# Inverse row sums turned together with the row maxima, from batch two on

## The chip, the cores and the metric

One core of a Trainium2 chip runs the kernel. The metric is the device time of one execution in microseconds (us). The core has five engines that work in their own order and wait for each other by semaphores: TensorE (PE in the rows, its weight loads PEld), VectorE (DVE), ScalarE (ACT), GpSimd (POOL) and SyncE (SP), which issues the transfers.

## The reference

Four batches of 512 tokens with 512 channels go through one layer: causal cross attention to a 128-wide context (16 heads in 4 groups, 32 wide), and then a mixture of eight units with a shared branch. The attention is what the change touches:

```python
scores = jnp.einsum('bgnqd,bgkd->bgnqk', qg, k) * scale
scores = jnp.where(causal, scores, -1e30)
attn = jax.nn.softmax(scores, axis=-1)
out = jnp.einsum('bgnqk,bgkd->bgnqd', attn, v)
out = out.reshape(B, N_HEADS, T, hd).transpose(0, 2, 1, 3).reshape(B, T, C)
return out @ w_out.T
```

## The kernel before, in words

The attention is cut into 32 spans `u`: batch `b` (4), half of the queries `h` (2), key group `kv` (4). A span has 4 heads (`G`) of 256 queries (`Q`), which is 2 tiles of 128 queries per head. Spans 0 to 7 are the first batch, 8 to 31 the other three.

Each engine runs one hand-written loop over the same 288 slots `s`, from -40 to 247. In every slot it issues its share of that slot's work in a fixed order. `span_slot(u)` is the slot at which span u starts. From batch two on a span takes 4 slots when h is 0 and 8 or 9 when h is 1. Nearly all slots from 32 on also hold one "filler": one 128 x 512 product of the mixture, of the output projection or of the down projection, in two parts of six or more fp32r matmuls, and two PSUM banks (`u_bank`) take turns at them.

Softmax is done in two passes. In the first pass (`pass_a`, line 1510) queries are the rows: in the slots of the span before u, DVE takes each row's maximum (`row_max`, 1227) and ACT the exponentials' row sums (`row_sum`, 980). In the second pass (`pass_b`, 1534) keys are the rows, and the negated maxima must stand along the queries as two more rows of `q_st`. So

- DVE splits the maxima into a high and a low fp32r part (`maxima_split`, 1236 and 1238, into `mhl`) at slot `span_slot(u) - 1`;
- PE turns them (`maxima_turn`, 1490) at slot `span_slot(u)`, behind the first part of the filler and the slot's `pass_a` products, and ahead of the filler's second part;
- ACT copies them to `m_t` (`maxima_out`, 972), and SP carries them to `q_st` (`rows`), which the second pass reads from slot `span_slot(u) + 3`.

The inverse row sums scale the value products, whose rows are 32 channels of each of 4 heads. So

- DVE takes the reciprocal (`inverse`, 1244) near the end of slot `span_slot(u)`;
- POOL spreads each head's value over 32 columns (`spread_inverse`, 872, into `rrep`) one slot later;
- PE turns both 128 x 128 tiles (`inverse_turn`, 1499) first thing in slot `span_slot(u) + 5`, and ACT copies them to `r_t` (`inverse_out`, 987), for DVE's `attended` (1253).

Small products share a ring of three PSUM banks (`short_products`): one may start when the bank's reader three products ago is done.

In a slot DVE's order is: the first row maximum, the low part of a turned tile (1205), the evacuation of the filler of slot s - 1 (`gate` with 1366 and 1387 for a unit, `residual` ending in 1266, or `finish`, 1398), the other row maxima, and then all else. The gate waits for ACT's tanh of the same filler (1048). ACT's tanh of the filler of slot s - 1 stands early in its slot s, behind all of its slot s - 1, which ends with `weights_high` (945).

Of the kernel before, what the change touches and what calls it, by code (L numbers as in the profile page):

```python
# [70 lines left out]
def attention_and_mixture_kernel(nc, x, ctx_in, q_norm_w, k_norm_w, w_out, w_router, w_units, w_down,  # L71
# [38 lines left out]
    U0 = 3  # L110
    POOL_LOW = (3,)

    f32 = lambda ap: ap.bitcast(F32)
# [6 lines left out]
    with common:  # L120
# [42 lines left out]
        wt = sb("wt", [P, NT, NK])  # L163
        st2, mv2, ln2 = sb("st2", [P, NT, 6]), sb("mv2", [P, NT, 2]), sb("ln2", [P, 4, NT])
        mixs, amp = sb("mixs", [NE, NK]), sb("amp", [NE, NK, 2])
# [25 lines left out]
        def sem(name):  # L191
# [31 lines left out]
        s_pa, s_max, s_sum, s_mhi, s_mlo, s_mt, s_mout = (sem(n) for n in (  # L223
            "pass_a", "row_max", "row_sum", "max_high", "max_low", "max_turned", "max_out"))
        s_rinv, s_rrep, s_rt1, s_rout = (sem(n) for n in (
            "row_inverse", "inverse_spread", "inverse_turned", "inverse_out"))
# [73 lines left out]

        def of_span(s, name):
# [265 lines left out]
        def short_products(s):  # L567

            found = []
            if (u := of_span(s, "inverse_turn")) is not None:  # L570
# [72 lines left out]
        def sync_engine(e):  # L643
# [48 lines left out]
            def rows(u):  # L692
                e.wait_ge(s_mout, u - KV + 1)
                if u >= QR:
                    e.wait_ge(*queries_read(u - QR))
                for k in range(2):
                    e.dma_start(f32(q_st[MAXROW + k:MAXROW + k + 1, u % QR, :, :]),
                                f32(m_t[k * G:(k + 1) * G, :])).then_inc(s_m[u % 2], 16)

# [61 lines left out]
        def pool_engine(e):  # L761
            e.memset(half_neg[:], -0.5).then_inc(s_small, 1)
            e.memset(ident[:], 0.0)
# [4 lines left out]
            e.affine_select(out=ident[:], in_=ident[:], compare_op=ALU.not_equal, fill=1.0, base=0,  # L768
                            pattern=[[-1, P]], channel_multiplier=1)
# [98 lines left out]
            def spread_inverse(u):  # L868
                e.wait_ge(s_rinv, u + 1)
                if u >= 1:  # L870
                    e.wait_ge(s_rt1, u)
                e.tensor_copy(heads(rrep[:]), rinv[:, u % 2].unsqueeze(3).broadcast_to([P, TH, G, D])
                              ).then_inc(s_rrep, 1)

            def mask_probabilities(u, k):

# [32 lines left out]
            for s in slots:  # L909
                if (step := second_pass_step(s - SELECT)) is not None:  # L910
                    mask_probabilities(*step)
                if (hb := of_half(s, "query_scale")) is not None:
                    query_scale(hb)
                if (u := of_span(s, "spread")) is not None:
                    spread_inverse(u)
# [26 lines left out]
        def scalar_engine(e):  # L942
# [25 lines left out]
            def maxima_out(u):  # L968
                e.wait_ge(s_mt, u - KV + 1)
                if u > KV:  # L970
                    e.wait_ge(*max_rows(u - 1))
                e.activation(m_t[:], short("maxima", u - KV)[0:2 * G, 0:Q], ACT.Copy).then_inc(s_mout, 1)

# [94 lines left out]
            for s in slots:  # L1068
# [4 lines left out]
                for n in tiles_in(s, "turn"):  # L1073
                    high(n)
                if (u := of_span(s, "inverse_turn")) is not None:
                    inverse_out(u)
# [33 lines left out]
        def vector_engine(e):  # L1110
# [119 lines left out]
            def maxima_split(u):  # L1230
                r = u % 2
                hi, lo = mhl[:, r, :, 0:G], mhl[:, r, :, G:2 * G]
                e.wait_ge(s_max, (u + 1) * G * TH)
# [22 lines left out]
            def residual(f):  # L1256
# [6 lines left out]
                e.wait_ge(s_x1, n + 1)  # L1263
                e.bn_stats(st2[:, n, :], xs).then_inc(s_bn2, 1)
                e.wait_ge(s_bn2, n + 1)
                e.bn_aggr(mv2[:, n, :], st2[:, n, :]).then_inc(s_agg2, 1)

# [139 lines left out]
            for s in slots:  # L1407
# [39 lines left out]
                for g in moments_in(s):  # L1447
                    moments(g)
                if (u := of_span(s, "inverse")) is not None:
                    inverse(u)  # L1450
# [9 lines left out]
        def tensor_engine(e):  # L1460
# [3 lines left out]
            def turn_in(n):  # L1464
# [4 lines left out]
                for t in range(TH):  # L1469
                    last = e.transpose(bank[:, t * P:(t + 1) * P], r1_b[:, n % 2, t, :], ident[:])  # L1470
                last.then_inc(s_turn, 1)

            def turn_stacked(n):
# [3 lines left out]
                for i, done in enumerate((s_turn_a, s_turn)):  # L1477
                    e.wait_ge(*stack_free(n, i))
                    for j in range(2):
                        for t in range(TH):  # L1480
                            copies = r3[:, n % 2, t * G + 2 * i + j].rearrange("p c d -> p (c d)")
                            last = e.transpose(stack_banks(n)[i][0:MAXROW, j * Q + t * P:j * Q + (t + 1) * P], copies, ident[:])
                    last.then_inc(done, 1)

            def maxima_turn(u):
                e.wait_ge(s_mlo, u - KV + 1)
                e.wait_ge(*short_free("maxima", u - KV))
                bank = short("maxima", u - KV)
                for t in range(TH):
                    last = e.transpose(bank[0:2 * G, t * P:(t + 1) * P], f32(mhl[:, u % 2, t, :]), ident[:])  # L1490
                last.then_inc(s_mt, 1)

            def inverse_turn(u):

                e.wait_ge(s_rrep, u + 1)
                e.wait_ge(*short_free("inverse", u))
                bank = short("inverse", u)
                for t in range(TH):
                    last = e.transpose(bank[:, t * P:(t + 1) * P], rrep[:, t, :], ident[:])
                last.then_inc(s_rt1, 1)  # L1500
# [12 lines left out]
            def turn_probabilities(u, k):  # L1513
# [4 lines left out]
                for j in range(G):  # L1518
                    for t in range(k, TH):
                        at = j * w + t * P - seen(u, k)  # L1520
                        last = e.transpose(pair[:, at:at + P], masked_scores(u, j * TH + t)[:, k * P:(k + 1) * P], ident[:])
                last.then_inc(s_pb, 1)
# [30 lines left out]
            def turn_x(n):  # L1553
# [3 lines left out]
                for k in range(KC):  # L1557
                    last = e.transpose(bank[:, k * P:(k + 1) * P], xn[:, k * P:(k + 1) * P], ident[:])  # L1558
                last.then_inc(s_xt, 1)
# [13 lines left out]
            def turn_choice(p):  # L1573
# [3 lines left out]
                for t in range(2):  # L1577
                    last = e.transpose(bank[:, t * P:(t + 1) * P], cf[:, t, 0:NE], ident[:])
                last.then_inc(s_cft, 1)
# [10 lines left out]
            def turn_down(g):  # L1590
# [6 lines left out]
                for h in range(2):  # L1597
                    e.wait_ge(*short_free("down", 2 * g + h))
                    bank = short("down", 2 * g + h)
                    for k in range(ND // 2):  # L1600
                        last = e.transpose(bank[:, k * P:(k + 1) * P], blocks[h * (ND // 2) + k], ident[:])  # L1601
                    last.then_inc(s_dt, 1)
# [70 lines left out]
            for s in slots:  # L1673
                if (u := of_span(s, "inverse_turn")) is not None:
                    inverse_turn(u)
# [101 lines left out]
```

## Time and profile before

| | |
|---|---|
| median of 3 runs | 809.68 us (809.2 to 809.68) |
| the profiled execution's own time | 809.42 us |
| its span, first to last instruction | 807.7 us |
| PE busy | 763.8 us, 95% |
| PE weight loads | 608.0 us, 75% |
| DVE busy | 646.1 us, 80% |
| ACT busy | 578.0 us, 72% |
| POOL busy | 532.5 us, 66% |
| mean granted TensorE clock | 0.987 of 2.4 GHz |

Busy time is that of an engine with an instruction at work; for PE the ends of matmuls are modelled and overlap the next one's start, so the time from start to start says what one costs.

### The profile page before, as it was taken

To read this page: it belongs to the slowest core of one execution; us is meant where nothing else is said; L and a number is where in the kernel's file an instruction comes from. 1 tells how busy PE (TensorE), PEld (TensorE's weight loads), DVE (VectorE), ACT (ScalarE), POOL (GpSimd) and SP (SyncE) were. 2 spreads that over 40 slices of the span, in tenths; PEclk is the share of its full clock that TensorE was granted. 3 is DMA by queue.
4 is the path that set the end of the run, shared out by engine and by line. 5 is a ranking of instruction groups with operands and counts; after the bars stand their busy time and mean duration, and the time that the engine had idled before them with its cause. 6 is when DMAs were issued, how large, how long until landed. Compare 5 with 4: busy or idle time off the path is not lost. (4 is left out here: it accounts for less than half of the span.)

```text
span 807.7 us, 15292 instructions
## 1 busy us (share of the span) xinstructions
PE 763.8 (95%) x4180; PEld 608.0 (75%) x4180; DVE 646.1 (80%) x1635; ACT 578.0 (72%) x1413; POOL 532.5 (66%) x685
## 2 busy tenths in 40 slices
PE   2768799999999999999999999999999999999998
PEld 2545577777777878777778778777778887788886
DVE  7767787889788877889788787888788887688774
ACT  3878796788777867788778767787777775655552
POOL 4586489784697769775687849777465615662572
PEclk9979999999999999999999999999999999999999
DMA  8323144554545446545455445554545335454650
GB/s 291 122 68 97 41 134 161 179 166 138 192 156 172 153 141 220 194 154 178 146 175 179 141 157 181 170 164 135 197 150 173 136 125 185 157 188 133 207 201 35
DMA packets 57052, 127.03 MB, mean 157 GB/s; under 512 B 10920, under 2 KB 28040, under 8 KB 56968
## 3 DMA queue, kind: packets, MB, share of 16 engines
q1 hardware_dynamic: 56968, 126.04, 47.3%
q8 instruction: 36, 0.59, 0.3%
q14 instruction: 48, 0.39, 0.2%
HBM read 107.55 MB, written 4.46 MB: 139 GB/s over the span
## 5 line engine op out<-in xcount | busy, mean ns | idle before, releaser
L1634 PE MATMUL u<-w_h,t_h 128*128 128x512 f32 x640 | 258.4, 404 | 1.1 <-issue 0.8
L1634 PE MATMUL u<-w_l,t_h 128*128 128x512 f32 x640 | 251.2, 393 | 0.0
L1634 PE MATMUL u<-w_h,t_l 128*128 128x512 f32 x640 | 251.0, 392 | 0.0
L1284 DVE TENSOR_TENSOR w_l<-w_raw,w_h 128x512 fp32r<-128x512 f32 x288 | 240.4, 861 | 0.3 <-ACT w_h L945 0.3
L945 ACT ACTIVATE w_h<-w_raw 128x512 fp32r<-128x512 f32 x384 | 219.0, 621 | 7.9 <-DMA w_raw<-in_w_units 7.0
L899 POOL TENSOR_TENSOR w_l<-w_raw,w_h 128x512 fp32r<-128x512 f32 x96 | 139.1, 1449 | 101.8 <-ACT w_h L945 101.8
L980 ACT ACTIVATE scores<-scores,mx 128x384 f32<-128x384 f32 (+1 forms) x224 | 128.8, 575 | 70.4 <-DVE mx L1227 69.2
L907 POOL TENSOR_TENSOR macc<-macc,gb 128x256 f32<-128x256 f32 x112 | 106.1, 951 | 58.9 <-DVE gb L1387 58.4
L1634 PEld LDWEIGHTS u<-w_h,t_l 128*128 128x128 f32 x640 | 120.6, 188 | 26.9
L1227 DVE CUSTOM_DVE_ANT_0 scores<-s,mask_qk 128x384 f32<-128x384 f32 (+1 forms) x224 | 112.4, 503 | 35.5 <-PE s L1510 34.9
L1634 PEld LDWEIGHTS u<-w_h,t_h 128*128 128x128 f32 x640 | 121.0, 189 | 25.8 <-issue 3.0
L1634 PEld LDWEIGHTS u<-w_l,t_h 128*128 128x128 f32 x640 | 121.3, 190 | 20.1
L1510 PE MATMUL s<-k_st,q_st 96*128 96x384 f32 (+1 forms) x248 | 88.1, 366 | 8.2 <-DVE mx L1227 3.9
L998 ACT ACTIVATE pr<-pair 128x1024 f32<-128x1024 f32 x88 | 77.7, 883 | 21.1 <-PE pair L1534 20.6
L1366 DVE SCALAR_TENSOR_TENSOR th<-th,u 128x256 f32<-128x256 f32 x160 | 66.5, 416 | 31.9 <-ACT th L1048 30.0
L1048 ACT ACTIVATE th<-u 128x256 f32<-128x256 f32 x160 | 60.2, 376 | 36.2 <-PE u L1634 35.6
L882 POOL TENSOR_SCALAR_AFFINE_SELECT pr<-pr 128x512 f32<-128x512 f32 x56 | 47.2, 843 | 36.8 <-ACT pr L998 36.8
L1387 DVE SCALAR_TENSOR_TENSOR gb<-th,wt,u 128x256 f32<-128x256 f32 x112 | 53.9, 481 | 16.0
L1510 PEld LDWEIGHTS s<-k_st,q_st 96*128 96x128 f32 x248 | 48.2, 199 | 22.9 <-issue 14.8
L1534 PE MATMUL pair<-q_st,k_st 98*128 98x512 f32 x148 | 51.0, 410 | 2.0 <-ACT pr L998 2.0
L1549 PE MATMUL o_bank<-pr,ct 128*32 128x256 f32 (+1 forms) x768 | 42.6, 363 | 0.0
L980 ACT ACTIVATION_READ_ACCUMULATOR scores<-scores,mx 128x1 f32 x224 | 42.5, 190 | 0.0
(152 smaller groups left out, 1175.0 us busy)
## 6 DMA issues: line engine op xcount, KB each, us to landing
w_raw<-in_w_units SPq DMA_DIRECT2D x160, 512.0 KB, 4.2
w_raw<-in_w_out_t SPq DMA_DIRECT2D x16, 512.0 KB, 5.1
w_raw<-in_shared_w_down SPq DMA_DIRECT2D x16, 512.0 KB, 4.6
q_st<-turned_h SPq DMA_DIRECT2D x224, 32.0 KB, 2.8
out<-x SPq DMA_DIRECT2D x16, 256.0 KB, 2.2
q_st<-turned_l SPq DMA_DIRECT2D x112, 32.0 KB, 2.7
x<-in_x SPq DMA_DIRECT2D x3, 1024.0 KB, 9.2
k_st<-turned_h SPq DMA_DIRECT2D x48, 32.0 KB, 2.8
```

Source lines behind the costliest of these rows:

```text
L899: e.tensor_tensor(w_l[:, i % WR, k, :], w_raw[:, i % WR, k, :], f32(w_h[:, i % WR, k, :]), ALU.subtract).then_inc(s_wlp, 1)
L907: e.tensor_tensor(total, total, gb[:, adds_before(w, g) % 2, :], ALU.add).then_inc(s_acc, 1)
L945: e.activation(w_h[:, i % WR, k, :], w_raw[:, i % WR, k, :], ACT.Copy).then_inc(s_wh, 1)
L980: e.activation(s, s, ACT.Exp, bias=mx[:, u % 2, t, j:j + 1], scale=-1.0, accum_out=sums[:, u % 2, t, j:j + 1]).then_inc(s_sum, 1)
L998: e.activation(pr[:, n % PR, 0:width], pair[:, 0:width], ACT.Exp, scale=-1.0).then_inc(s_ex, 1)
L1048: e.activation(th[:, n % 2, :], u_bank[filler_no[f] % 2][:, 0:I], ACT.Tanh, scale=0.5).then_inc(s_tanh, 1)
L1227: e.tensor_tensor_reduce(masked_scores(u, m), scores_bank(i)[:, 0:width], mask_qk[:, T - width:T], 1.0, 3e38, ALU.add, ALU.min, mx[:, u % ...
L1284: e.tensor_tensor(w_l[:, i % WR, k, :], w_raw[:, i % WR, k, :], f32(w_h[:, i % WR, k, :]), ALU.subtract).then_inc(s_wl, 1)
L1366: e.scalar_tensor_tensor(th[:, n % 2, :], th[:, n % 2, :], 1.0, up, ALU.add, ALU.mult).then_inc(s_ga, 1)
L1387: e.scalar_tensor_tensor(to, th[:, n % 2, :], scale, gate_v, ALU.mult, ALU.mult).then_inc(s_gb, 1)
L1510: e.matmul(scores_bank(i)[:, 0:w], q_st[0:MAXROW, u % QR, j, t * P:(t + 1) * P], k_st[0:MAXROW, (b * KV + kv) % KR, 0:w], start=True, stop ...
L1634: last = e.matmul(u_bank[n % 2][:], t[:, k, cols], ww[:, i % WR, k, :], start=(k == 0 and m == 0), stop=(k == KC - 1 and m == 2))
```

## The change

Spans 0 to 7 keep the spread and the turn of full tiles. For spans 8 to 31:

- `mhl` is 16 wide: high and low part of the inverses (`hi`, `lo`, 4 columns each) stand ahead of those of the maxima. DVE does the reciprocal and then two more operations (`inverse_split`), now right behind the evacuation of the filler in slot `span_slot(u)`, ahead of the slot's other row maxima.
- `maxima_turn` waits for that split too and turns all 16 columns. For all spans from 4 on it is now an ordinary fp32r matmul with the unit matrix in place of a transposition. `maxima_out` copies 16 rows.
- `inverse_turn` is one fp32r matmul of a constant 0/1 matrix (`chooser`, 8 x 128) with the first 8 rows of `m_t`, at slot `span_slot(u) + 3` in place of + 5.
- POOL makes `chooser` once, in slot 53, and copies no more inverses. `st2` shrinks to two entries, with a wait.

```diff
+INVERSE_ROWS, CHOOSER_SLOT = 3, 53
+    SPREAD = H * KV
-        mhl, m_t = sb("mhl", [P, 2, TH, 2 * G], F32R), sb("m_t", [2 * G, Q], F32R)
-        rrep, r_t = sb("rrep", [P, TH, P]), sb("r_t", [P, 2, Q])
+        mhl, m_t = sb("mhl", [P, 2, TH, 4 * G], F32R), sb("m_t", [4 * G, Q], F32R)
+        chooser, r_t = sb("chooser", [P, TH, P], F32R), sb("r_t", [P, 2, Q])
-        ident = sb("ident", [P, P])
+        ident_r = sb("ident", [P, P], F32R)
+        ident = f32(ident_r[:])
...
+        def inverse_rows_in(s):
+            for u in range(SPREAD, NU):
+                if s == span_slot(u):
+                    return u
+            return None
+        def inverse_turn_in(s):
             for u in range(NU):
-                if s == span_slot(u) + core(u, name):
+                if s == span_slot(u) + (core(u, "inverse_turn") if u < SPREAD else INVERSE_ROWS):
                     return u
...
+            def make_chooser():
+                e.wait_ge(s_rt1, SPREAD)
+                rows = chooser[0:2 * G, 0, :]
+                e.memset(f32(rows), 0.0).then_inc(s_chooser, 1)
...
+                e.affine_select(out=by_head(rows), in_=by_head(f32(rows)), compare_op=ALU.not_equal, fill=1.0, base=0,
+                                pattern=[[-1, G], [0, D]], channel_multiplier=1).then_inc(s_chooser, 1)
...
             def maxima_out(u):
+                if u > SPREAD:
+                    e.wait_ge(s_rt1, u)
+                made = 2 * G if u < SPREAD else 4 * G
+                e.activation(m_t[0:made, :], short("maxima", u - KV)[0:made, 0:Q], ACT.Copy).then_inc(s_mout, 1)
...
             def inverse(u):
                 e.wait_ge(s_sum, (u + 1) * G * TH)
                 if u >= 2:
-                    e.wait_ge(s_rrep, u - 1)
+                    e.wait_ge(*((s_rrep, u - 1) if u - 2 < SPREAD else (s_isplit, 2 * (u - 1 - SPREAD))))
                 e.reciprocal(rinv[:, u % 2], sums[:, u % 2]).then_inc(s_rinv, 1)
+            def inverse_split(u):
+                r = u % 2
+                hi, lo = mhl[:, r, :, 0:G], mhl[:, r, :, G:2 * G]
+                e.wait_ge(s_rinv, u + 1)
+                if u >= KV + 2:
+                    e.wait_ge(s_mt, u - KV - 1)
+                e.tensor_copy(hi, rinv[:, r]).then_inc(s_isplit, 1)
+                e.wait_ge(s_isplit, 2 * (u - SPREAD) + 1)
+                e.tensor_tensor(lo, rinv[:, r], f32(hi), ALU.subtract).then_inc(s_isplit, 1)
...
                     evict[fillers[s - 1][0]](fillers[s - 1])
                 if s == START[0]:
                     mixture_table()
+                if (u := inverse_rows_in(s)) is not None:
+                    inverse(u)
+                    inverse_split(u)
                 for u, m in first_pass_tiles(s)[1:]:
                     row_max(u, m)
...
             def maxima_turn(u):
                 e.wait_ge(s_mlo, u - KV + 1)
+                if u >= SPREAD:
+                    e.wait_ge(s_isplit, 2 * (u - SPREAD) + 2)
+                first = 2 * G if u < SPREAD else 0
                 e.wait_ge(*short_free("maxima", u - KV))
                 bank = short("maxima", u - KV)
                 for t in range(TH):
-                    last = e.transpose(bank[0:2 * G, t * P:(t + 1) * P], f32(mhl[:, u % 2, t, :]), ident[:])
+                    last = e.matmul(bank[0:4 * G - first, t * P:(t + 1) * P], mhl[:, u % 2, t, first:4 * G], ident_r[:],
+                                    start=True, stop=True)
                 last.then_inc(s_mt, 1)
             def inverse_turn(u):
+                if u >= SPREAD:
+                    e.wait_ge(s_chooser, 3)
+                    e.wait_ge(s_mout, u - KV + 1)
+                    e.wait_ge(*short_free("inverse", u))
+                    e.matmul(short("inverse", u)[:, 0:Q], chooser[0:2 * G, 0, :], m_t[0:2 * G, :],
+                             start=True, stop=True).then_inc(s_rt1, 1)
+                    return
```

## Rows read from the trace of the kernel before

**Rows 1.** Stretch of batches two to four: busy us (x instructions) by engine, clock, DMA.

```profile
134.00:690.00 556.00, 551.79 (x3072) 442.63 (x3073) 462.55 (x1174) 421.32 (x1037) 385.85 (x480) 1.00 0.50 165
```

**Rows 2.** PE's longest wait in that stretch: us in total, times, longest.

```profile
PE s L1601 <- DVE mx L1227: 1.5, 3, 0.6
```

**Rows 3.** Timeline, spans 8, 16, 17, 18, 31: start us, duration us; filler's evacuation, maxima's turn.

```profile
136.32 0.38 PE L1490 MATMUL s<-ident,mhl 128*8 128x128 f32 x2
136.86 0.48 DVE L1387 SCALAR_TENSOR_TENSOR gb<-th,wt,u 128x256 f32<-128x256 f32 x1
...
323.25 0.48 DVE L1387 SCALAR_TENSOR_TENSOR gb<-th,wt,u 128x256 f32<-128x256 f32 x1
325.05 0.38 PE L1490 MATMUL s<-ident,mhl 128*8 128x128 f32 x2
...
338.14 0.38 PE L1490 MATMUL s<-ident,mhl 128*8 128x128 f32 x2
338.97 0.48 DVE L1387 SCALAR_TENSOR_TENSOR gb<-th,wt,u 128x256 f32<-128x256 f32 x1
...
352.10 0.38 PE L1490 MATMUL s<-ident,mhl 128*8 128x128 f32 x2
353.22 0.48 DVE L1387 SCALAR_TENSOR_TENSOR gb<-th,wt,u 128x256 f32<-128x256 f32 x1
...
676.83 0.48 DVE L1387 SCALAR_TENSOR_TENSOR gb<-th,wt,u 128x256 f32<-128x256 f32 x1
677.01 0.38 PE L1490 MATMUL s<-ident,mhl 128*8 128x128 f32 x2
```

**Rows 4.** Timeline of ACT ahead of span 18's turn.

```profile
350.87 1.15 ACT L945 ACTIVATE w_h<-w_raw 128x512 fp32r<-128x512 f32 x2
...
352.18 0.39 ACT L1048 ACTIVATE th<-u 128x256 f32<-128x256 f32 x1
```

**Rows 5.** Timeline of DVE: the two splitting operations of span 18's maxima.

```profile
350.17 0.17 DVE L1236 TENSOR_SCALAR mhl<-mx 128x8 fp32r<-128x8 f32 x1
350.38 0.17 DVE L1238 SCALAR_TENSOR_TENSOR mhl<-mx,mhl 128x8 fp32r<-128x8 f32 x1
```

**Rows 6.** Groups by line, shapes apart: busy us, mean ns of one, idle before and releaser.

```profile
L1238 DVE SCALAR_TENSOR_TENSOR mhl<-mx,mhl 128x8 fp32r<-128x8 f32 x28 | 11.2, 400 | 1.0
...
L1236 DVE TENSOR_SCALAR mhl<-mx 128x8 fp32r<-128x8 f32 x28 | 9.4, 337 | 0.5
...
L1244 DVE RECIPROCAL rinv<-sums 128x8 f32<-128x8 f32 x32 | 6.2, 195 | 1.4 <-ACT early L980 1.3
```

**Rows 7.** The same view of POOL.

```profile
L872 POOL COPY rrep<-rinv 128x256 f32<-128x256 f32 x32 | 17.3, 539 | 15.4 <-DVE rinv L1244 15.0
```

**Rows 8.** The same view of PE: the 128-column fp32 value products.

```profile
L1549 PE MATMUL o_bank<-pr,ct 128*32 128x128 f32 x256 | 13.6, 286 | 0.0
```

**Rows 9.** Timeline of PE: two products of a filler; two transpositions, then products.

```profile
405.83 0.39 PE L1634 MATMUL u<-w_l,t_h 128*128 128x512 f32 x1
406.06 0.39 PE L1634 MATMUL u<-w_h,t_l 128*128 128x512 f32 x1
...
406.74 0.38 PE L1470 MATMUL s<-ident,r_b 128*128 128x128 f32 x2
406.88 0.48 PE L1634 MATMUL u<-w_h,t_h 128*128 128x512 f32 x1
407.20 0.40 PE L1634 MATMUL u<-w_l,t_h 128*128 128x512 f32 x1
```

**Rows 10.** Timeline of PE: a 256-column fp32r product and the next.

```profile
334.16 0.28 PE L1510 MATMUL s<-k_st,q_st 96*128 96x256 f32 x1
334.28 0.39 PE L1534 MATMUL pair<-q_st,k_st 98*128 98x512 f32 x1
```

**Rows 11.** Two stretches of the first batch, columns as in the first group.

```profile
71.00:77.60 6.60, 5.32 (x32) 3.39 (x34) 5.42 (x16) 5.63 (x13) 3.65 (x9) 1.00 0.49 177
77.60:81.10 3.50, 3.50 (x34) 1.92 (x27) 2.20 (x6) 2.71 (x8) 3.00 (x8) 0.51 0.22 57
```

More of the change, by code:

```diff
@@ L140, in attention_and_mixture_kernel @@
         mx, sums, rinv = (sb(n, [P, 2, TH, G]) for n in ("mx", "sums", "rinv"))
-        mhl, m_t = sb("mhl", [P, 2, TH, 2 * G], F32R), sb("m_t", [2 * G, Q], F32R)
-        rrep, r_t = sb("rrep", [P, TH, P]), sb("r_t", [P, 2, Q])
+        mhl, m_t = sb("mhl", [P, 2, TH, 4 * G], F32R), sb("m_t", [4 * G, Q], F32R)
+        with ExitStack() as before:
+            rrep = before.enter_context(nc.sbuf_tensor("rrep", [P, TH, P], F32))
+        chooser, r_t = sb("chooser", [P, TH, P], F32R), sb("r_t", [P, 2, Q])
         o_h = sb("o_h", [P, KV, T], F32R)
         mask_qk = sb("mask_qk", [P, T])
-        ident = sb("ident", [P, P])
+        ident_r = sb("ident", [P, P], F32R)
+        ident = f32(ident_r[:])
         w_h, wd_h = sb("w_h", [P, WR, KC, 2 * I], F32R), sb("wd_h", [P, KD, C], F32R)
@@ L299, in maxima_in, with of_spread_span @@
             return u if u is not None and (u < H * KV) == first else None
-        def of_span(s, name):
+        def of_spread_span(s, name):
+            for u in range(SPREAD):
+                if s == span_slot(u) + core(u, name):
+                    return u
[3 more added lines that the diff above has]
+                if s == span_slot(u):
+                    return u
+            return None
+        def inverse_turn_in(s):
             for u in range(NU):
-                if s == span_slot(u) + core(u, name):
+                if s == span_slot(u) + (core(u, "inverse_turn") if u < SPREAD else INVERSE_ROWS):
                     return u
@@ L569, in short_products @@
             found = []
-            if (u := of_span(s, "inverse_turn")) is not None:
+            if (u := inverse_turn_in(s)) is not None:
                 found.append(("inverse", u))
@@ L695, in rows @@
                     e.wait_ge(*queries_read(u - QR))
+                first = 0 if u < SPREAD else 2 * G
                 for k in range(2):
                     e.dma_start(f32(q_st[MAXROW + k:MAXROW + k + 1, u % QR, :, :]),
-                                f32(m_t[k * G:(k + 1) * G, :])).then_inc(s_m[u % 2], 16)
+                                f32(m_t[first + k * G:first + (k + 1) * G, :])).then_inc(s_m[u % 2], 16)
             def store(g):
@@ L873, in spread_inverse @@
                               ).then_inc(s_rrep, 1)
+            def make_chooser():
+                e.wait_ge(s_rt1, SPREAD)
+                rows = chooser[0:2 * G, 0, :]
+                e.memset(f32(rows), 0.0).then_inc(s_chooser, 1)
+                by_head = lambda ap: ap.rearrange("p (j d) -> p j d", d=D)
+                e.wait_ge(s_chooser, 1)
+                e.affine_select(out=by_head(rows), in_=by_head(f32(rows)), compare_op=ALU.not_equal, fill=1.0, base=0,
+                                pattern=[[-1, G], [0, D]], channel_multiplier=1).then_inc(s_chooser, 1)
+                e.wait_ge(s_chooser, 2)
+                e.affine_select(out=by_head(rows), in_=by_head(f32(rows)), compare_op=ALU.not_equal, fill=1.0, base=-G,
+                                pattern=[[-1, G], [0, D]], channel_multiplier=1).then_inc(s_chooser, 1)
             def mask_probabilities(u, k):
@@ L913, in pool_engine @@
                     query_scale(hb)
-                if (u := of_span(s, "spread")) is not None:
+                if s == CHOOSER_SLOT:
+                    make_chooser()
+                if (u := of_spread_span(s, "spread")) is not None:
                     spread_inverse(u)
@@ L1074, in scalar_engine @@
                     high(n)
-                if (u := of_span(s, "inverse_turn")) is not None:
+                if (u := inverse_turn_in(s)) is not None:
                     inverse_out(u)
@@ L1231, in maxima_split @@
                 r = u % 2
-                hi, lo = mhl[:, r, :, 0:G], mhl[:, r, :, G:2 * G]
+                hi, lo = mhl[:, r, :, 2 * G:3 * G], mhl[:, r, :, 3 * G:4 * G]
                 e.wait_ge(s_max, (u + 1) * G * TH)
@@ L1448, in vector_engine @@
                     moments(g)
-                if (u := of_span(s, "inverse")) is not None:
+                if (u := of_spread_span(s, "inverse")) is not None:
                     inverse(u)
@@ L1469, in turn_in @@
                 for t in range(TH):
-                    last = e.transpose(bank[:, t * P:(t + 1) * P], r1_b[:, n % 2, t, :], ident[:])
+                    last = e.transpose(bank[:, t * P:(t + 1) * P], r1_b[:, n % 2, t, :], ident)
                 last.then_inc(s_turn, 1)
@@ L1481, in turn_stacked @@
                             copies = r3[:, n % 2, t * G + 2 * i + j].rearrange("p c d -> p (c d)")
-                            last = e.transpose(stack_banks(n)[i][0:MAXROW, j * Q + t * P:j * Q + (t + 1) * P], copies, ident[:])
+                            last = e.transpose(stack_banks(n)[i][0:MAXROW, j * Q + t * P:j * Q + (t + 1) * P], copies, ident)
                     last.then_inc(done, 1)
@@ L1498, in inverse_turn @@
                 for t in range(TH):
-                    last = e.transpose(bank[:, t * P:(t + 1) * P], rrep[:, t, :], ident[:])
+                    last = e.transpose(bank[:, t * P:(t + 1) * P], rrep[:, t, :], ident)
                 last.then_inc(s_rt1, 1)
@@ L1520, in turn_probabilities @@
                         at = j * w + t * P - seen(u, k)
-                        last = e.transpose(pair[:, at:at + P], masked_scores(u, j * TH + t)[:, k * P:(k + 1) * P], ident[:])
+                        last = e.transpose(pair[:, at:at + P], masked_scores(u, j * TH + t)[:, k * P:(k + 1) * P], ident)
                 last.then_inc(s_pb, 1)
@@ L1557, in turn_x @@
                 for k in range(KC):
-                    last = e.transpose(bank[:, k * P:(k + 1) * P], xn[:, k * P:(k + 1) * P], ident[:])
+                    last = e.transpose(bank[:, k * P:(k + 1) * P], xn[:, k * P:(k + 1) * P], ident)
                 last.then_inc(s_xt, 1)
@@ L1577, in turn_choice @@
                 for t in range(2):
-                    last = e.transpose(bank[:, t * P:(t + 1) * P], cf[:, t, 0:NE], ident[:])
+                    last = e.transpose(bank[:, t * P:(t + 1) * P], cf[:, t, 0:NE], ident)
                 last.then_inc(s_cft, 1)
@@ L1600, in turn_down @@
                     for k in range(ND // 2):
-                        last = e.transpose(bank[:, k * P:(k + 1) * P], blocks[h * (ND // 2) + k], ident[:])
+                        last = e.transpose(bank[:, k * P:(k + 1) * P], blocks[h * (ND // 2) + k], ident)
                     last.then_inc(s_dt, 1)
@@ L1673, in tensor_engine @@
             for s in slots:
-                if (u := of_span(s, "inverse_turn")) is not None:
+                if (u := inverse_turn_in(s)) is not None:
                     inverse_turn(u)
```

14 lines of the change are left out of this document (8 added, 6 removed).

## The prediction

> **What bounds the kernel now.** I read the table of stretches first, for the stretch in which spans 8 to 31 run. PE is at work for 551.8 of 556 us at full clock, while DVE has 462.6, ACT 421.3 and POOL 385.9 [rows 1]. The waits of PE come next: its longest in this stretch are three for a row maximum, 1.5 us together, 0.6 the longest [rows 2]. So PE sets the pace from 134 to 690 us. What another engine saves there is worth nothing, what PE saves is worth its start-to-start time, and whatever makes PE wait is added nearly whole, because PE has no idle time in which to take it back.
>
> The view that decides is the timeline around PE's turn of the maxima, since that is where the change adds a wait. The kernel before turns them as soon as PE comes to them; their split was made a slot earlier. What is new must wait for DVE to reach a later place in its queue: the evacuation of the filler of slot s - 1.
>
> **The new wait.** In slot `span_slot(u)` DVE now does, in this order: evacuate the last filler, reciprocal, copy, subtract. PE's turn in the same slot needs the last of them. Behind the turn in PE's queue stand the second-pass product of the slot and the second part of the filler, and everything after; none can pass.
>
> How late is DVE? At span 18 PE starts the turn at 352.10, and DVE's gate of the last filler runs from 353.22 to 353.70, 1.60 us behind PE's start [rows 3]. The reason is ACT: it makes two high parts of weights from 350.87 to 352.02, and its tanh of that filler starts only at 352.18, after PE had come to the turn [rows 4]. In the kernel before this lateness costs nothing, because only the next use of the filler's bank depends on it.
>
> From the gate's end the chain is: reciprocal 0.20 us [rows 6], then copy and subtract. Neither is in the trace on the inverses, but the maxima's split is the same pair of shapes: 0.17 each when undisturbed [rows 5], 0.34 and 0.40 in the mean [rows 6]. Between the two lie 0.04 us (350.17 + 0.17 to 350.38) [rows 5]; I take this for each of three hand-overs, the last to PE. That gives 0.20 + 0.34 + 0.12 = 0.66 at least and 0.20 + 0.74 + 0.12 = 1.06 with mean durations. I take 0.85.
>
> So PE's wait at a span is the evacuation's end + 0.85 - the turn's start, or nothing where that is negative [rows 3]:
> - span 8: 136.86 + 0.48 + 0.85 - 136.32 = 1.87
> - span 16: 323.25 + 0.48 + 0.85 - 325.05 < 0, nothing
> - span 17: 338.97 + 0.48 + 0.85 - 338.14 = 2.16
> - span 18: 353.22 + 0.48 + 0.85 - 352.10 = 2.45
> - span 31: 676.83 + 0.48 + 0.85 - 677.01 = 1.15
>
> The other 19 spans, read the same way, follow this pattern: spans 8 to 11, 17 to 19 and 25 to 27 wait 1.5 to 2.7, spans 12, 20 and 28 wait 0.8, spans 29 to 31 about 1.2, and the other eight 0.13 or nothing. The sums over the 24 pairs of such rows, from the first at 136.32 to the last at 677.01, are 8.8 us in batch two, 7.3 in three and 11.3 in four: 27.4. With a chain of 0.66 it is 24, with 1.06 about 32.
>
> Does a wait at one span make the next shorter, because ACT and DVE catch up? Partly. Span 16 has DVE in time and span 17, four slots later, has it late again by the full amount [rows 3]: the lateness is rebuilt within a span by the order in the slots, and is not a backlog carried from before. I take a tenth off, an estimate, for what ACT and DVE make up: 24.6 us.
>
> **PE's own work.** The time from start to start is the price. Two transpositions of 128 x 128 and one 512-column product take 407.20 - 406.74 = 0.46 us, and the product by itself takes 406.06 - 405.83 = 0.23: 0.115 for a transposition [rows 9].
> - Removed: 24 spans x 2 transpositions of `rrep` x 0.115 = 5.5 us.
> - Added: 24 products with the 0/1 matrix, 256 fp32r columns, 334.28 - 334.16 = 0.12 each [rows 10]: 2.9 us.
> - Changed: 28 x 2 = 56 turns of `mhl`, transpositions at 0.115, become fp32r products of 128 columns. No row shows such a product. Below it is bounded by half of the 256-column row, 0.06 [rows 10]; above by the fp32 value products of the same 128 columns, four of which run side by side in 13.6 / 64 = 0.21 us [rows 8]. Operands and width are those of the transpositions, so I keep their 0.115, and the term is nothing. The ends are 56 x (0.06 - 0.115) = -3.1 and 56 x (0.21 - 0.115) = +5.3 us.
>
> Together PE's work is 2.6 us less, between -5.7 and +2.7.
>
> The Trainium skill ("FP8 and Floating Point Precision", section "TensorE Precision Notes") says that a true fp32 product takes four passes through the array and that reduced precision reads 4 bytes and truncates. By one pass the new turns would cost the lower bound above, and the sum would be 3.1 us lower; no row here shows a narrow fp32r product, so the sum does not go by it.
>
> **What costs nothing.** POOL loses 24 copies of 0.54 us [rows 7] and gains three small operations in slot 53; it has 170 us idle in the stretch [rows 1], and before it no one waited for its copy at PE. DVE gains 48 operations of 0.17 to 0.40 us, up to 18 us in all, in its 93 idle us [rows 1]; uncovered, they are already in the wait's chain. They stand ahead of the slot's other row maxima, whose bank PE needs three small products later, and PE itself is later by then. ACT copies 16 rows in place of 8 with the same 256 columns. Nothing waits anew on SP: its two transfers of maxima rows wait for `maxima_out` as before, and the second pass that reads them stands three slots further on, over 10 us, so that neither they nor the weight loads behind them in SP's queue come late. The move of `inverse_turn` from slot + 5 to + 3 shifts the ring of banks by one place in two slots of each span; PE's three waits there of at most 0.6 [rows 2] say what such a collision costs, so I put at most 24 x 0.1 = 2.4 us in the range and nothing in the sum.
>
> **The sum.** 24.6 - 2.6 = +22.0 us on the profiled execution's 809.4 (its span of 807.7 and 1.7 around it) is 831.4; the median of the runs is 0.3 higher than that execution, so 831.7, say 832.
>
> **Rivals.**
> - *The clock falls too*, chance 0.2. In the first batch the granted clock went from 2.4 to 1.2 GHz for 3.5 us after 6.6 us in which PE worked 5.32, that is with 1.3 us idle [rows 11]. The new waits put up to 2.7 us of idle time into such a stretch, so some could bring a fall. Each costs half of 3.5 us, 1.7 us; with a fall at 6 of the 10 spans with waits over 1.5 us it is +10: 842. Against it, PE works at full density between the waits, which it did not in the first batch. The Trainium skill ("TensorE: Matmul & The Clock Gate", section "HAM oscillation — how this bites in real kernels") tells of kernels that lose the fast clock at each pause between dense groups; the trace has such falls only in the first batch.
> - *The lateness is a backlog*, chance 0.15: each wait lets ACT and DVE catch up and the next spans find them nearer. If half of the 27.4 us goes so, the time is 809.7 + 13.7 - 2.6 = 821. Span 17 speaks against it.
> - *Faster*, chance 0.04: the first waits, some 2 us, clear the lateness for good, and PE's work saves its lower bound 5.7; 809.7 + 2 - 5.7 = 806. It decides from the point at which all waits together are under the saving, 2.6 us in the middle case. At span 18 alone the wait is 2.45, so this needs ACT's tanh to move by over a microsecond at nearly all ten places.
> - *Waits and saving cancel*, chance 0.03: 809 to 811.
>
> **How the numbers follow.** The forecast has the remaining 0.58. Its own range takes the wait's ends (24 and 32, less a tenth: 21.6 to 28.8), PE's ends (-5.7 to +2.7) and the ring's 2.4: 809.7 + 15.9 = 825.6 to 809.7 + 33.9 = 843.6. The range for 8 in 10 reaches down to most of the backlog case and takes in the clock case's middle: 819 to 846. A difference of 0.2%, 1.6 us, is about what a measurement of this kernel can tell from none. Faster by more has 0.04, within it 0.03, slower 0.93.
>
> **What would show it.** In the changed kernel PE's waits should have a new first line: the turn of `mhl` waits for DVE's split of the inverses, about 18 times and 25 us in all, the longest near 2.5 us, at spans 9, 10, 17, 18, 25 and 26, and nearly none at 13, 15, 16, 21, 23 and 24. The stretch of batches two to four should be some 22 us longer with PE's idle time up by as much. Start-to-start times of the new 128-column turns would show 0.06, 0.115 or 0.21. Granted clock under 1.00 in that stretch would be the first rival; waits that shrink after the first span of a batch, the second. The prediction is wrong if DVE reaches the split less than a microsecond behind PE at most spans.

## The result and the profile after

The changed kernel takes 840.94 us (median of 6 runs, 839.29 to 844.64) against 809.68 (6 runs, 807.14 to 810.28): ratio 1.0403, 95% interval 1.0387 to 1.0418. The profiled execution took 840.38 us, its span is 838.7, 31.0 more than before. The forecast was 832, range 819 to 846, slower with 0.93. So the time lies in the range, 9 us above the forecast.

The stretch table of the changed kernel has the same columns as [rows 1]. It goes on to 720 us, where the changed kernel has done the work that the kernel before had done at 690:

```profile
134.00:720.00 586.00, 560.59 (x3049) 440.90 (x3048) 476.42 (x1219) 422.22 (x1036) 366.20 (x458) 1.00 0.48 156
```

PE was idle for 4 us of its stretch in [rows 1]; here it is idle for 25. The waits of PE over the whole span (us in total, times, longest) name the place:

```profile
PE s L1549 <- issue: 25.1, 16, 2.5
...
PE s L1577 <- DVE mx L1268: 3.2, 5, 1.3
```

L1549 is the turn of `mhl`. The view puts the wait down to "issue", that is to nothing that it could name. One version of the kernel (e4, below, which differs in the rows of another product) has the same waits, and for two of them its view names the releaser; L1296 is the subtraction in `inverse_split`:

```profile
PE s L1550 <- DVE mhl L1296: 5.0, 2, 2.5
```

The timelines of PE and DVE at span 18 of the changed kernel say the same. They answer to the fourth pair of rows in [rows 3] and to [rows 5]:

```profile
363.18 0.28 PE L1577 MATMUL s<-k_st,q_st 96*128 96x256 f32 x1
365.82 0.37 PE L1549 MATMUL s<-ident,mhl 128*16 128x128 f32 x2 [2.36 <-issue]
365.99 0.73 PE L1601 MATMUL pair<-q_st,k_st 98*128 98x512 f32 x1
```

```profile
363.53 0.42 DVE L1246 TENSOR_TENSOR turned_l<-s,turned_h 128x256 fp32r<-128x256 f32 x1 [1.46 <-ACT turned_h L998]
363.87 0.41 DVE L1419 SCALAR_TENSOR_TENSOR th<-th,u 128x256 f32<-128x256 f32 x1
364.43 0.48 DVE L1440 SCALAR_TENSOR_TENSOR gb<-th,wt,u 128x256 f32<-128x256 f32 x1
364.83 0.20 DVE L1285 RECIPROCAL rinv<-sums 128x8 f32<-128x8 f32 x1
365.06 0.24 DVE L1293 CAST mhl<-rinv 128x8 fp32r<-128x8 f32 x1
365.33 0.39 DVE L1295 TENSOR_TENSOR mhl<-rinv,mhl 128x8 fp32r<-128x8 f32 x1
```

DVE's gate ends at 364.91 and its subtraction at 365.72. The turn starts at 365.82, which is 0.91 us behind the gate's end, where 0.85 was assumed. Before the turn PE stands idle from the end of the score product to that moment.

A wait's idle time is a little less than what it costs, since a matmul's modelled end lies behind the moment at which the next could have started. The cost is the time from the start of the product ahead of the turn to the start of the turn: 365.82 - 363.18 = 2.64 here. Added over spans 8 to 31 it is 32.6 us in the changed kernel and 5.6 in the kernel before, 27.1 more.

The product with the 0/1 matrix at span 19, with its neighbours and two of the weight loads (PEld):

```profile
397.79 0.39 PE L1722 MATMUL u<-w_h,d_l 128*128 128x512 f32 x1
398.11 0.18 PEld L1559 LDWEIGHTS s<-m_t,chooser 8*128 8x128 f32 x1 [0.36 <-issue]
398.11 0.38 PE L1559 MATMUL s<-m_t,chooser 8*128 8x256 f32 x1
398.42 0.19 PEld L1577 LDWEIGHTS s<-k_st,q_st 96*128 96x128 f32 x1
398.42 0.44 PE L1577 MATMUL s<-k_st,q_st 96*128 96x384 f32 x1
398.70 0.40 PE L1722 MATMUL u<-wd_h,d_h 128*128 128x512 f32 x1
```

It starts 0.32 us behind the product before it, which alone takes 0.23, and the next starts 0.31 behind it, where 0.12 was forecast [rows 10]. Its weights and those of the next are loaded only as each product starts. Adding up start-to-start differences between the two kernels around the 24 old and the 24 new places of the inverse turn gives +5.7 us, where the forecast had 2.9 - 5.5 = -2.6. How far behind each place one counts matters a little: up to the second product behind it, the sum is +5.4, of which the 24 new products are 11.6 and the removed transpositions -6.2.

The two products of each new turn start 0.06 us apart, the lower bound of the forecast. But the products behind them come later by most of what this saves: from the start of a turn to the second product behind it the two kernels differ by 0.01 us in the mean. That is 0.3 us in all, and 1.0 us in a version without the wait (e12, below).

From 134 us to the last products the granted clock fell once, to 1.2 GHz, right at a wait. Stretch, busy us by engine, clock, DMA share, GB/s:

```profile
365.60:369.00 3.40, 3.18 (x9) 2.62 (x10) 2.20 (x5) 2.49 (x6) 3.26 (x6) 0.50 0.95 305
```

An estimate: 3.4 us at half the clock cost half of them, 1.7. Over the whole of a run, the mean granted clock was 0.988 in the fastest of the six (839.29 us) and 0.978 in the slowest (844.64 us).

### The profile page after: what moved, and what is told of

Read it like the earlier page. It is cut to its first block, busy times and chain, and to the rows that moved or that the text cites. A ratio compares the mean times of both kernels' runs of the same rounds, so it can differ in the third digit from the quotient of the medians.

```text
span 838.7 us, 15287 instructions
## 1 busy us (share of the span) xinstructions
PE 774.6 (92%) x4156; PEld 607.5 (72%) x4156; DVE 660.5 (79%) x1683; ACT 580.2 (69%) x1413; POOL 514.5 (61%) x664
## 4 chain that ended last, share of the span: by engine, by line
PE 83%; issue 5%; ACT 3%; DVE 2%; POOL 2%; DVEq 0%; POOLq 0%; ACTq 0%
PE u L1701 50%; PE u L1722 8%; PE u L1685 5%; PE s L1577 5%; PE o_bank L1616 4%; PE pair L1601 4%; PE s L1636 2%; PE s L1668 1%; PE s L1559 1%; PE s L1549 1%; PE s L1526 1%; ACT scores L1021 1%; PE s L1625 1%; ACT w_h L983 1%; POOL macc L943 0%
## 5 line engine op out<-in xcount | busy, mean ns | idle before, releaser
L935 POOL TENSOR_TENSOR w_l<-w_raw,w_h 128x512 fp32r<-128x512 f32 x96 | 136.7, 1424 | 125.1 <-ACT w_h L983 125.1
L943 POOL TENSOR_TENSOR macc<-macc,gb 128x256 f32<-128x256 f32 x112 | 104.2, 932 | 80.2 <-DVE gb L1440 80.2
L918 POOL TENSOR_SCALAR_AFFINE_SELECT pr<-pr 128x512 f32<-128x512 f32 x56 | 44.6, 796 | 49.7 <-ACT pr L1039 49.7
```

What stands on the lines that cost most here:

```text
L935: e.tensor_tensor(w_l[:, i % WR, k, :], w_raw[:, i % WR, k, :], f32(w_h[:, i % WR, k, :]), ALU.subtract).then_inc(s_wlp, 1)
L943: e.tensor_tensor(total, total, gb[:, adds_before(w, g) % 2, :], ALU.add).then_inc(s_acc, 1)
```

## The experiments

**The dose: where the split stands in VectorE's slot.** If the wait at the turn is the cause, the time must follow its size. So two versions of the changed kernel make it smaller (e1) and larger (e2), and only this place differs.

```diff
+                if (u := inverse_rows_in(s)) is not None:      # e1: ahead of the evacuation
+                    inverse(u)
+                    inverse_split(u)
                 if s - 1 in fillers:
                     evict[fillers[s - 1][0]](fillers[s - 1])
-                if (u := inverse_rows_in(s)) is not None:
-                    inverse(u)
-                    inverse_split(u)
                 for u, m in first_pass_tiles(s)[1:]:
                     row_max(u, m)
```

> Only the place of the reciprocal and the split in VectorE's slot is changed: ahead of the filler's evacuation in place of behind it. If TensorE's wait is set by VectorE's queue (my theory), the evacuation's 1 us no longer lies in the chain: read from the rows of before, the waits at the turn fall from 27 us to about 12 and the time is 841 - 15 = 826. If the lateness is a backlog that moves with the work (rival), or if the waits only stand for something else, the time stays within 3 us of 841.

Measured: 825.92 us, ratio to before 1.0205 (1.0181 to 1.0229), as expected.

e2 has the three lines behind the loop over `row_max`.

> The opposite dose: reciprocal and split behind the slot's other row maxima. My theory: the chain grows by a row maximum (0.35 to 0.7 us) at the spans in whose slot another row maximum stands there, some 12 to 16 of 24: 841 + 6, 845 to 850. Rival (the wait is not the cause): 841.

Measured: 852.7 us, ratio 1.0513 (1.0468 to 1.0559), which is over the range of the expectation.

The wait at the turn, in e1 and then in e2:

```profile
PE s L1549 <- issue: 9.7, 10, 1.8
```

```profile
PE s L1549 <- issue: 30.2, 18, 2.8
```

Moving three small operations by one item in DVE's queue moves the time by 15 us one way and 12 the other, with the idle time at the turn (25.1, 9.7, 30.2) in step. In e2 part of the rise is the clock: from batch two on the records show 1.2 GHz for 17 us in four places, each at or right behind a wait, as in the stretch below. The one run of e2 with a mean granted clock of 0.988 took 846.3 us; the other three had 0.970 to 0.976 and took 852.6 to 852.9.

```profile
370.50:377.30 6.80, 6.13 (x17) 4.88 (x18) 3.38 (x8) 2.88 (x7) 5.34 (x7) 0.50 0.44 149
```

**The wait alone taken away.** In e12 every span's turn takes the split of the span before it, which is long done. So each span is scaled with the wrong row sums, but all the work is there, at its place.

```diff
-                hi, lo = mhl[:, r, :, 0:G], mhl[:, r, :, G:2 * G]
+                hi, lo = mhl[:, o, :, 0:G], mhl[:, o, :, G:2 * G]     # o = (u + 1) % 2
...
-                if u >= KV + 2:
-                    e.wait_ge(s_mt, u - KV - 1)
+                e.wait_ge(s_mt, u - KV)
...
-                if u >= SPREAD:
-                    e.wait_ge(s_isplit, 2 * (u - SPREAD) + 2)
+                if u > SPREAD:
+                    e.wait_ge(s_isplit, 2 * (u - SPREAD))
```

> The wait alone is taken away: VectorE writes the split of a span's inverses for the turn of the next span, so that every span is scaled with the inverse row sums of the one before (the values are not the reference's); every instruction, its place and its engine stay as in the changed kernel, 8-row product included. If the wait at the turn is the cause, its 27 us and the clock's fall go: 841 less 27 to 29 is 812 to 814, what remains being the few-row products (+5.7) less old waits. Rival (the work that was added costs by itself): over 825.

Measured: 822.2 us, ratio 1.0160 (1.0143 to 1.0177). The wait at the turn from span 8 on is gone and so is the clock's fall, but the time falls by 18.7 us and not by 27 to 29: neither the expectation nor its rival. A line of PE's waits in e12, us in total, times, longest:

```profile
PE s L1669 <- DVE mx L1269: 3.9, 3, 1.4
```

These are the transpositions ahead of the down projection, which wait for a row maximum that reads their bank; before they had 1.5 us [rows 2]. DVE's three operations stand ahead of that row maximum. In the changed kernel the list of PE's waits has no such line (there it would be L1668): while PE stood at the turn, DVE and ACT caught up. So the wait at the turn covered some 10 us of other lateness (its 27.1 us and the 1.7 of the clock, less 18.7). Matching the products of the two traces one by one shows 4.4 us of it at these transpositions and 1.7 at those of normalized rows.

**The number of rows of the 0/1 product.** In e4 it is 128 in place of 8, and in e5 it is 32. The rows added to `chooser` and `m_t` are zero.

```diff
-                    e.matmul(short("inverse", u)[:, 0:Q], chooser[0:2 * G, 0, :], m_t[0:2 * G, :],
+                    e.matmul(short("inverse", u)[:, 0:Q], chooser[0:128, 0, :], m_t[0:128, :],
```

> The product with the 0/1 matrix runs over 128 rows, the added ones zero, in place of 8. The trace shows its weights not loaded ahead: 0.32 us from the product before, 0.31 to the next. If the few rows are the reason (my theory), the product costs about 0.12 as other 256-column ones, 0.2 to 0.35 us less at 24 places: 832 to 836. If it is its place in the queue, its semaphore wait or the small stationary matrix made by GpSimd (rival), the time stays at 841.

Measured: 839.43 us, ratio 1.0367 (1.0343 to 1.0391), against 1.0403 for the change in another set of runs. This lies between what my theory and its rival said, and as a time it is unclear. The timeline of e4 at the place of span 19 is not:

```profile
399.51 0.39 PE L1723 MATMUL u<-w_h,d_l 128*128 128x512 f32 x1
399.51 0.19 PEld L1560 LDWEIGHTS s<-m_t,chooser 128*128 128x128 f32 x1
399.73 0.28 PE L1560 MATMUL s<-m_t,chooser 128*128 128x256 f32 x1
399.82 0.19 PEld L1578 LDWEIGHTS s<-k_st,q_st 96*128 96x128 f32 x1
399.85 0.41 PE L1578 MATMUL s<-k_st,q_st 96*128 96x384 f32 x1
```

The two distances are 0.22 and 0.12 us in place of 0.32 and 0.31, and each weight load now starts while the product before is at work. The same sum of start-to-start differences is -1.9 us against the kernel before, where it was +5.7 (to the second product behind each place, -3.2 where it was +5.4). What the profiled execution of e4 saved here it lost to the clock, which was at 1.2 GHz for 17 us from batch two on, in place of 3.4.

> As the run with 128 rows, but over 32. There the product's neighbours closed up and the cost of all moved inverse turns went from +5.7 us to -1.9 against the kernel before. If any product with fewer rows than its neighbours makes its weights wait, the 32-row product starts 0.32 us after the one before and its successor 0.31 later, as with 8 rows; if only odd, very small counts do, it closes up as with 128 (0.23 and 0.12).

Measured: 841.47 us (one run). The distances are 0.32 and 0.32 again, as with 8 rows:

```profile
398.78 0.39 PE L1723 MATMUL u<-w_h,d_l 128*128 128x512 f32 x1
399.10 0.38 PE L1560 MATMUL s<-m_t,chooser 32*128 32x256 f32 x1
399.42 0.44 PE L1578 MATMUL s<-k_st,q_st 96*128 96x384 f32 x1
```

The clean measure of the rows in time is the pair without the wait: e13 is e12 with 128 rows.

> The same, with the 0/1 product over 128 rows. Both causes gone, what the change saves on TensorE is left: 809.5 less 2 to 4 us, 805 to 808. If that saving is not real, 809 to 811.

Measured: 815.05 us, ratio 1.0073 (1.0053 to 1.0092): 7.1 us under e12. But it is not under the kernel before, as I had expected. Two experiments look for what is left, 5.7 us.

**The split's place once more.** e14 is e13 with the three DVE lines at the end of the slot, where `inverse` stood before.

> As the run with the inverses of the span before and 128 rows (815.1), but reciprocal and split stand near the end of VectorE's slot, where the reciprocal stood in the kernel before. In the trace of that run TensorE waits 1.4 us three times for a row maximum that the split now precedes. If the split's place explains part of what was left over the kernel before, the time falls by 2 to 4 us to 811 to 813; if it is the splitting work itself, or only the earlier place of the 0/1 product, it stays at 815.

Measured: 817.18 us, ratio 1.0088 (1.0071 to 1.0105), not to be told from e13. The place of the split does not explain the rest. One part of the rest is in the trace of e13 (and equally of e14). ACT's copy of the inverses to `r_t`, which frees a bank, now stands just ahead of the transposition of normalized rows that wants this bank:

```profile
352.06 0.28 PE L1579 MATMUL s<-k_st,q_st 96*128 96x256 f32 x1
352.62 0.36 ACT L1030 ACTIVATE r_t<-s 128x256 f32<-128x256 f32 x1
353.12 0.63 PE L1627 MATMUL s<-ident,xn 128*128 128x128 f32 x4 [0.79 <-ACT r_t L1030]
```

It occurs three times and costs 2.4 us of idle time, against 0.7 for the like waits before.

**The tiles' declarations.** All versions of the change had one thing more in common: in the stretch of batches two to four the 512-column products of a filler are 231.6 to 231.8 ns apart in the mean of some 1,400, and 230.5 in the kernel before; the commonest value is 229 in place of 227. So e15 is the kernel before with the change's declarations alone. Tiles behind `mhl` lie at other addresses; the unit matrix is declared fp32r, and the smaller `st2` needs its wait:

```diff
-        mhl, m_t = sb("mhl", [P, 2, TH, 2 * G], F32R), sb("m_t", [2 * G, Q], F32R)
-        rrep, r_t = sb("rrep", [P, TH, P]), sb("r_t", [P, 2, Q])
+        mhl, m_t = sb("mhl", [P, 2, TH, 4 * G], F32R), sb("m_t", [4 * G, Q], F32R)
+        with ExitStack() as before:
+            rrep = before.enter_context(nc.sbuf_tensor("rrep", [P, TH, P], F32))
+        chooser, r_t = sb("chooser", [P, TH, P], F32R), sb("r_t", [P, 2, Q])
...
-        st2, mv2, ln2 = sb("st2", [P, NT, 6]), sb("mv2", [P, NT, 2]), sb("ln2", [P, 4, NT])
+        st2, mv2, ln2 = sb("st2", [P, 2, 6]), sb("mv2", [P, NT, 2]), sb("ln2", [P, 4, NT])
```

> The kernel before with only the tile declarations of the change (mhl 16 wide, rrep's place shared with an unused chooser, the unit matrix declared fp32r, st2 of two entries with its wait), so that all tiles behind them lie at other SBUF addresses. Every version of the change has its filler products 1.2 ns further apart (231.7 ns in place of 230.5 in the stretch of batches two to four, the commonest value 229 in place of 227), some 3 us over 2,200 products. If the addresses are the cause, this kernel shows 231.7 ns and 811 to 813 us; if the cause is the changed work around them, 230.5 and 809.5.

Measured: 813.09 us, ratio 1.0055 (1.0036 to 1.0074), 3.9 us over the kernel before and at the upper end of what was expected, with the products 231.4 ns apart and 229 the commonest value. An estimate: 0.9 ns at each of the 2,400 such products is 2.2 us, so the spacing carries over half of the 3.9. That it is the addresses, and not the other type or the added wait, is likely but not shown. The table of a stretch shows the same at a coarser grain; first the kernel before, then e15: 1,588 matmuls begin in 290 us, and 1,584, at equal busy time.

```profile
400.00:690.00 290.00, 288.89 (x1588) 232.12 (x1587) 237.45 (x581) 215.30 (x514) 190.94 (x231) 1.00 0.48 160
```

```profile
400.00:690.00 290.00, 288.92 (x1584) 231.10 (x1583) 237.68 (x580) 215.19 (x514) 191.44 (x230) 1.00 0.49 161
```

**Versions meant to be fast.** e3 leaves DVE alone and turns one slot later.

> From span 8 on the turn of maxima and inverses stands one slot later (its copy and its transfers too), all else as in the changed kernel. My theory: VectorE is 2.7 us late at most and a slot has 3.5, so the wait is gone, 27 us, and the fall of the clock with it: 812 to 815. What is left over the kernel before, 3 to 5 us, is then the product with the 0/1 matrix. Rival: the wait comes back elsewhere, at the second pass that reads the transferred rows, and the time stays over 820.

Measured: 836.68 us, ratio 1.0335 (1.0312 to 1.0358). The expectation failed: the time stayed over 820, as the rival had it, though at another place than the rival named. The turn waits no more, but it has moved in the ring of three banks, and PE now waits for row maxima; waits of e3 in us in total, times, longest:

```profile
PE s L1668 <- DVE mx L1268: 9.6, 6, 2.5
PE s L1625 <- DVE mx L1268: 3.6, 3, 1.5
```

In its profiled execution the clock was at 1.2 GHz for 14 us, each time right behind one of the longest waits. e10 turns early in the next slot, with the split ahead of the evacuation and 128 rows.

> The split stands ahead of the evacuation (as in e1), the turn stands early in the next slot, behind its first pass_a product, some 1.9 us later than in the changed kernel, and the 0/1 product runs over 128 rows. The worst wait left in e1 was 1.8 us, so the turn's own wait should be gone: 809.3 - 2 + 0 to 3 = 807 to 811. Rival, by what the later turn showed: the order in the ring of three banks changes and TensorE waits for row maxima instead, some 10 us: 818 or more.

Measured: 824.21 us, ratio 1.0171 (1.0152 to 1.0189). This is the rival again: PE waits 5.6 us for row maxima ahead of the transpositions (3.7 and 1.9), and 3.3 us at the turn for its bank. e8 keeps the turn and puts the split at the very head of DVE's slot, with 128 rows.

> Reciprocal and split stand at the very head of VectorE's slot, ahead of the first row maximum and of the low part of the turned tile, and the 0/1 product runs over 128 rows. My theory: what is left of the wait is VectorE's first free moment in the slot (at span 18 of before 351.66) + 0.66 against TensorE's 352.10, 0.2 to 0.5 us at the ten worst spans, 3 to 5 in all; the 0/1 product now saves 1.9. 809.3 + 4 - 2 = 811, 809 to 814. Rival: the split now waits at the head for the last row sum and holds up VectorE's row maxima, for which TensorE then waits by its ring of banks: over 816.

Measured: 816.2 us, ratio 1.0079 (1.0067 to 1.0092), the fastest form of the change that scales every span with its own sums, and 24.7 us under the change. It is 2 us over the range, and at the mark of the rival. The trace bears the rival out in part:

```profile
PE s L1550 <- DVE mx L1269: 3.5, 6, 0.8
```

The turn now waits 3.5 us in all, as little as was expected, but for a row maximum that the split holds up and not for the split: at span 9 the split is done at 152.48 us, the row maximum at 152.83, and the turn starts at 152.97. The 3.9 us of the declarations, not known then, are in the time too. e9 is e8 with the 0/1 product one slot later.

> As the version with the split at the head of VectorE's slot and 128 rows (816.2), but with the product with the 0/1 matrix at slot + 4 in place of + 3, where no transposition of normalized rows follows it in the ring of banks; its copy by ScalarE held that up three times by 0.8 us. 814 if those waits go and none comes; 816 or more if they only change place.

Measured: 817.41 us, ratio 1.0102 (1.0087 to 1.0117). The waits only changed place: score products now wait 1.7 us for the copy to `r_t`. No version beat the kernel before.

## Why the prediction was right, and by what

**PE is the bound: right. A wait is added nearly whole: only in part.** PE's idle time in the stretch rose from 4 to 25 us. e1 and e2 move the time with the place of the split alone. But e12, without the wait, is only 18.7 us faster and not 27, for the reason given below.

**The 27.4 us from the rows: right.** Measured from start to start: 27.1. The places are those named: nothing at 13 to 15 and 21 to 23, the longest at 10, 18 and 26. Single spans were off by up to 0.4 us either way (less at 25, more at 29 to 31), so the closeness of the total is in part luck.

**A tenth off for catching up: wrong as a size and as an idea.** With the tenth off, the forecast had 24.6. At the turns nothing was made up: the tanh and the gate of the last filler are late by the order in the slot, as span 17 had said. What PE's standing still does give back is elsewhere: the small waits for row maxima and for `r_t` of the kernel before, and those which the change would have brought, fell away beneath it. That is why taking away 27 us of waits gave 18.7.

**PE's own work: the step that failed.** The prediction said 2.6 us less. Its term of 24 products with the 0/1 matrix at 0.12 us each was taken from a 256-column product of 96 rows. With 8 rows the weights are not loaded ahead, and a product costs some 0.48 us. The 24 moved turns cost 5.7 us more than the old ones in place of 2.6 less: 8.3 us off. With 128 rows they save 1.9 (e4), near the forecast. For the 128-column fp32r turns the lower bound held for their spacing, 0.06, but it was worth only 0.3 us in place of 3.1. The Trainium skill ("FP8 and Floating Point Precision", section "TensorE Precision Notes") gives a true fp32 product four passes through the array. Read as one pass for the reduced precision, which the page does not say outright, it agrees with the spacing of 0.06, but the sum by it would have been 3.1 us lower, and 0.3 was measured.

**A term that was missing:** the tiles' declarations, 3.9 us by e15 (3.2 in its profiled span).

**What was said to cost nothing.** POOL, SP and ACT's wider copy: no wait for any of them came up. DVE's operations ahead of the row maxima were not free where the stall did not hide them: 3.9 us at the down transpositions in e12, against 1.5. (In e14, with these operations at the slot's end, it is 2.5 us, but the time does not fall.)

**The sum.** 27.1 at the turns, 5.7 for the inverse turns and 1.7 for the clock are 34.5; the declarations (3.2 in the span) make it 37.7; the span rose by 31.0. Some 6.7 us went the other way. Matching the products of the two traces one by one shows 3.2 of them as old waits that fell away, at the transpositions ahead of the down projection (2.0) and of normalized rows (1.2). In the first 134 us the changed kernel is 1.1 us ahead; there the clock was at 1.2 GHz for 17.0 us in place of 20.4. How the other 2.4 divide is not settled.

**Luck.** Without these 6.7 us the time would have been some 847, outside the range of 819 to 846. The mechanism and its places were forecast and hold. That the errors of size (8.3 for the turns, 3.2 for the declarations, 2.5 for the tenth, 1.7 for the clock) stayed in the range is owed to waits that the prediction did not count.

**The rivals.** The clock did fall in the stretch, once in the profiled execution and for 17 us in those of e2 and e4; the runs of the change spread over 5.4 us where those before spread over 3.1. So the first rival was a part of the case and not an alternative, at a sixth of its price. That each fall began at a wait is what the traces show; that the waits cause them rests on their absence in e1, e8 and e12 from 134 us to the last products. The backlog rival is refuted by the waits' sizes at the turns, 2.4 to 2.8 us again in each batch. What DVE and ACT made up shows elsewhere, as said.

## What to carry to other kernels

When two results are packed into one instruction, it waits for the later of them: read from the trace where each producer stands in its engine's queue at that moment, and not how long the producer takes. The time from the consumer's start to the producer's end in the trace of before, summed over all places, gave the added waits to within 2% (single places to within 0.4 us), and a discount for catching up made it worse. And before a large wait is blamed for all of a loss, take it away alone: it hides smaller ones.

## What the runs showed of the hardware

- A matmul over 8 or 32 rows among ones over 96 and 128: its weight load starts with it and not ahead of it, and so does that of the next. 0.32 us behind the product before and 0.31 to 0.32 to the next, in place of 0.23 and 0.12 with zeros up to 128 rows; 7.1 us for 24 of them (e12, e13). Counts between 32 and 96 were not tried.
- fp32r products of 128 columns start 0.06 us apart, half of the 0.12 of 256-column ones; but over the two of a turn and the two products behind, this saved only 0.01 us against fp32 transpositions 0.11 apart (0.04 in e12).
- A change of the tiles' declarations (sizes, so addresses, and one type, with one wait added) moved the spacing of unchanged 512-column fp32r products from 230.5 to 231.4 ns in the mean, and the kernel by 0.55% (e15). Which of them matters was not tried.
- The granted clock fell to 1.2 GHz at single waits of 2.2 to 2.8 us in an otherwise dense stream, in some executions and at some waits only; e1 and e8, whose waits are 1.8 us and less, show no fall in batches two to four.
